# Cross attention with a mixture of experts: projection turns and VectorE's work moved between the steps, squares of the roots on GpSimd

## The reference

```python
q = layernorm(x) @ Wq.T ; k = context @ Wk.T ; v = context @ Wv.T      # (Wk and Wv interleave)
q, k = rmsnorm(q), rmsnorm(k)                                          # per head of 16
attn = softmax(einsum('bhnd,bhmd->bhnm', q, k) * 16 ** -0.5)
x = x + einsum('bhnm,bhmd->bhnd', attn, v)
x = x + moe_ffn(layernorm(x))
```

## Time and profile before

| what | value |
|---|---|
| runs of the kernel before | median 1047.12 us (1046.23 to 1047.95) |
| the profiled execution | 1044.72 us, its span 1043.0 us |
| TensorE's granted clock in it | 0.983 of full speed |
| busy over the span | PE 965.8, DVE 703.4, ACT 513.9, POOL 146.5 us |
| exponentials (L612), 128 of them | 240.5 us, mean 1879 ns |
| idle of ScalarE before them | 77.9 us, 75.1 of it ended by the scores |
| first exponential | at 41.97 us |
| MoE part | after the last unit, from about 488 us |

### The profile page before, as it was taken

The page is one execution under the profiler, slowest core; times in us unless marked ns, Lnnn a source line. Parts: engine busy times, 40 slices in busy tenths (PEclk is TensorE's granted clock), DMA queues, the critical chain, the costliest instruction groups (busy, mean ns, idle before and its releaser), DMA issues.

```text
span 1043.0 us, 17988 instructions
## 1 busy us (share of the span) xinstructions
PE 965.8 (93%) x6730; PEld 697.2 (67%) x6731; DVE 703.4 (67%) x1439; ACT 513.9 (49%) x625; POOL 146.5 (14%) x167
## 2 busy tenths in 40 slices
PE   4999999989998999976999999999999999999995
PEld 3534443345434453332998898889998998899895
DVE  6777867775687657663678675675666767757553
ACT  4577768856786568874333212422424232424211
POOL 1000000000000000001100000243233331332331
PEclk9999999999999999997899999999999999999998
DMA  9100100001000100201420118354363544553633
GB/s 336 69 1 2 41 1 1 16 6 61 1 2 21 62 1 1 102 21 41 140 83 21 41 36 270 74 180 71 62 181 71 164 83 151 131 137 69 174 61 40
DMA packets 28984, 78.93 MB, mean 76 GB/s; under 512 B 7040, under 2 KB 7040, under 8 KB 24832
## 3 DMA queue, kind: packets, MB, share of 16 engines
q1 hardware_dynamic: 18400, 52.31, 14.1%
q0 software_dynamic: 10528, 25.87, 12.7%
HBM read 57.64 MB, written 20.52 MB: 75 GB/s over the span
## 4 chain that ended last, share of the span: by engine, by line
PE 36%; DVE 8%; DMA 4%; issue 2%; ACT 1%; POOLq 0%; POOL 0%; SPq 0%; DVEq 0%; ACTq 0%
PE z_ps L1184 14%; PE u_ps L1184 10%; PE y_ps L1184 9%; DVE w_sb L1375 4%; PE xt_ps L1197 2%; DMA out<-y_sb,target 2%; DMA xg<-xn_dram,index 1%; DMA xn_dram<-dense 1%; DVE y_sb L1562 1%; DVE g_sb L1547 1%; DVE y_sb L1569 1%; DVE g_hi L1550 1%; DVE u_lo L1534 0%; PE z_ps L1178 0%; PE xt_ps L1210 0%
## 5 line engine op out<-in xcount | busy, mean ns | idle before, releaser
L612 ACT ACTIVATE probs<-scores 128x2048 f32<-128x2048 f32 x128 | 240.5, 1879 | 77.9 <-PE scores L267 75.1
L1184 PE MATMUL z_ps<-u_hi,w_sb 128*128 128x256 f32 x896 | 169.6, 287 | 6.6 <-DVE u_lo L1534 6.6
L1184 PE MATMUL u_ps<-x_hi,w_sb 128*128 128x256 f32 x896 | 167.5, 285 | 4.8 <-issue 3.0
L1313 ACT ACTIVATE u_hi<-u_ps,b_ug 128x256 fp32r<-128x256 f32 x112 | 47.1, 472 | 238.5 <-PE u_ps L1184 238.5
L1184 PEld LDWEIGHTS z_ps<-u_hi,w_sb 128*128 128x128 f32 x896 | 142.9, 193 | 8.1 <-DVE u_lo L1534 8.1
L1184 PEld LDWEIGHTS u_ps<-x_hi,w_sb 128*128 128x128 f32 x896 | 142.8, 193 | 7.6 <-issue 4.5
L1184 PE MATMUL y_ps<-w_sb,g_hi 128*128 128x512 f32 x448 | 138.7, 391 | 0.0
L283 PE MATMUL o_ps<-probs,v_sb 128*17 128x512 f32 x1024 | 137.3, 609 | 1.0 <-ACT probs L612 1.0
L1184 PE MATMUL z_ps<-u_lo,w_sb 128*128 128x256 f32 x448 | 127.4, 284 | 0.0
L1184 PE MATMUL u_ps<-x_lo,w_sb 128*128 128x256 f32 x448 | 127.4, 284 | 0.0
L267 PEld LDWEIGHTS scores<-q_st,k_hi 32*128 32x128 f32 x512 | 25.1, 183 | 124.0 <-ACT probs L612 70.5
(11 more groups left out here) (216 smaller groups left out, 1562.5 us busy)
## 6 DMA issues: line engine op xcount, KB each, us to landing
w_raw<-w_all SPq DMA_DIRECT2D x27, 1024.0 KB, 8.3
ctx_raw<-ctx_t SPq DMA_DIRECT2D x4, 1024.0 KB, 6.2
out<-x_sb SPq DMA_DIRECT2D x16, 256.0 KB
xg<-xn_dram POOLq DMA_DIRECT2D x14, 256.0 KB
x_sb<-x SPq DMA_DIRECT2D x1, 3072.0 KB, 18.7
xn_dram<-xn SPq DMA_DIRECT2D x12, 256.0 KB, 2.1
bd<-b_down SPq DMA_DIRECT2D x9, 256.0 KB
x_sb<-x SPq DMA_DIRECT2D x4, 256.0 KB, 3.5
```

The costliest lines, as they stand in the source:

```text
L612: nc.scalar.activation(probs[:, t % 2], scores[:], ACT.Exp).then_inc(p_ready, 1)
L1184: ins = nc.tensor.matmul(out_ps, stat[a], mov[b], start=(first and a + b == 0), stop=(last and a == 1), skip_group_check=True)
L1313: last = nc.scalar.activation(u_hi[:, c, :], u_ps[:, b, a, :], ACT.Identity, bias=b_ug[:, par, 0, c:c + 1])
```

## The change

TensorE: the turns of k are spread 5, 1, 4, 2 over steps 6, 7, 0, 1 and those of q 4, 5, 3 over steps 3, 4, 5. In step 6 of groups 1 to 3 of a batch with a follower the k turns stand behind `weighed`. ScalarE: `root2_q` and `root2_k` go to GpSimd as products; `square_q` goes from step 7 to 6; `norm_high` of tile 1 is gone (VectorE does `norm_both`). VectorE: `stack_q` of half 0 goes from step 3 to 4, of half 1 from step 4 to step 0 of the next unit; `newton_k` from 6 to 5; the parts of `context_split` from steps 2, 3, 4, 4 to 1, 2, 2, 3; the statistics of a coming batch from steps 0, 1, 6, 7 to 1, 2, 3, 6.

```diff
+        K_TURNS = {6: (0, 5), 7: (5, 6), 0: (6, 10), 1: (10, 12)}
+        Q_TURNS = {3: (0, 4), 4: (4, 9), 5: (9, 12)}
...
+            def root2_q(u):
+                pool.wait_ge(rq_ready, u + 1)
+                pool.wait_ge(norm_done, 2 * u if u else 1)
+                nc.gpsimd.tensor_tensor(r2[:], r0[:], r0[:], ALU.mult).then_inc(r2q_ready, 1)
+
+            def root2_k(u):
+                pool.wait_ge(rk_ready, u + 1)
+                if u:
+                    pool.wait_ge(norm_done, 2 * u + 1)
+                nc.gpsimd.tensor_tensor(r2[:], r0[:], r0[:], ALU.mult).then_inc(r2k_ready, 1)
+
             root(0, 0)
             nc.gpsimd.memset(xt2[:, 1], 0.0).then_inc(zeros_set, 1)
...
+            root2_k(0)
+            root2_q(0)
+            roots = 1
+            for u in range(UNITS):
+                b, g, more, behind = batch_of(u)
+                if u + 1 < UNITS:
+                    root2_q(u + 1)
+                if behind and g == 1:
+                    root(roots, 1)
+                    roots += 1
+                if u + 1 < UNITS:
+                    root2_k(u + 1)
...
+                if u == 0 or (g == GROUPS - 1 and b + 2 < BATCH):
+                    root(roots, 0)
+                    roots += 1
...
@@ def between(u, s): @@
+                if s in (0, 1) and u + 1 < UNITS:
+                    k_turns(u + 1, *K_TURNS[s])
...
-                elif s <= 5:
+                elif s in Q_TURNS:
                     if ahead:
-                        q_passes(u + 2, s - 3)
+                        q_turns(u + 2, *Q_TURNS[s])
...
-                    if ahead:
-                        k_chunk(u + 2, 0)
                     if behind and g == 2:
                         gates(b - 1, 0)
-                elif ahead:
-                    k_chunk(u + 2, 1)
+                    if ahead and not (more and g >= 1):
+                        k_turns(u + 2, *K_TURNS[s])
+                elif s == 7 and ahead:
+                    k_turns(u + 2, *K_TURNS[s])
                     sum_q(u + 2)
+
+            def after(u, s):
+                b, g, more, behind = batch_of(u)
+                if s == 6 and more and g >= 1:
+                    k_turns(u + 2, *K_TURNS[s])
...
@@ def before_exp(u, s): @@
                 elif s == 3:
-                    if nxt:
-                        root2_q(u + 1)
...
                 elif s == 6:
                     if more and g == 1:
                         norm_high(b + 1, 0)
-                    if nxt:
-                        root2_k(u + 1)
-                else:
-                    if more and g == 1:
-                        norm_high(b + 1, 1)
                     if u + 2 < UNITS:
                         square_q(u + 2)
...
@@ def step(u, s): @@
                 if s == 0:
-                    stat1(0)
+                    if more and g == 2:
+                        norm_both(b + 1, 2)
+                    if u:
+                        stack_q(u, 1)
                     if behind and g == 1:
                         stat(tile_of(b - 1, 2), mv2[:, 2, :])
...
                     if nxt:
                         first_root_q(u + 1)
-                elif s == 2:
                     if more and g == 2:
                         context_split(b + 1, 0)
+                    stat1(0)
+                elif s == 2:
                     if u:
                         finalize(u - 1, 1)
                     if nxt:
                         sums_k(u + 1)
+                    if more and g == 2:
+                        context_split(b + 1, 1)
+                        context_split(b + 1, 2)
...
                         newton_q(u + 1)
-                        stack_q(u + 1, 0)
                     if more and g == 2:
-                        context_split(b + 1, 1)
+                        context_split(b + 1, 3)
...
                         first_root_k(u + 1)
-                        stack_q(u + 1, 1)
+                        stack_q(u + 1, 0)
...
                     finalize(u, 0)
+                    if nxt:
+                        newton_k(u + 1)
...
                 elif s == 6:
                     if more and g == 1:
                         norm_low(b + 1, 0)
+                        norm_both(b + 1, 1)
                     if nxt:
-                        newton_k(u + 1)
                         stack_k(u + 1, 0)
...
                 else:
-                    if more and g == 1:
-                        norm_low(b + 1, 1)
...
```

More of the change, by code:

```diff
@@ L292, in three, with q_turns @@
                 return ins
-            def q_passes(u, part):
+            TURNS = [(c, a, b) for c in range(DC) for a, b in ((0, 0), (0, 1), (1, 0))]
+            def q_turns(u, first, end):
                 g = u % GROUPS
-                if part == 0:
+                if first == 0:
                     begin("b", B_AT, ("q", u), b_free)
@@ L299, in q_passes @@
                     pe.wait_ge(xt_split, (u // GROUPS + 1) * BT)
-                turns = [(c, a, b) for c in range(DC) for a, b in ((0, 0), (0, 1), (1, 0))]
-                for c, a, b in turns[4 * part:4 * part + 4]:
+                for c, a, b in TURNS[first:end]:
                     last = nc.tensor.matmul(bank_b[:], (wq_hi, wq_lo)[a][:, g, c, :], (xt_hi, xt_lo)[b][:, c, :],
@@ L304, in q_passes, with k_turns @@
                                             skip_group_check=True)
-                if part == 2:
+                if end == len(TURNS):
                     last.then_inc(b_ready, 1)
-            def k_chunk(u, c):
+            def k_turns(u, first, end):
                 g = u % GROUPS
-                if c == 0:
+                if first == 0:
                     begin("a", A_AT, ("k", u), a_free)
@@ L313, in k_chunk @@
                     pe.wait_ge(ctx_split, (u // GROUPS + 1) * MT)
-                last = three(bank_a[:], (wk_hi[:, g, c, :], wk_lo[:, g, c, :]), (ctx_hi[:, c, :], ctx_lo[:, c, :]),
-                             c == 0, c == DC - 1)
-                if c == DC - 1:
+                for c, a, b in TURNS[first:end]:
+                    last = nc.tensor.matmul(bank_a[:], (wk_hi, wk_lo)[a][:, g, c, :], (ctx_hi, ctx_lo)[b][:, c, :],
+                                            start=(c == 0 and a + b == 0), stop=(c == DC - 1 and a == 1),
+                                            skip_group_check=True)
+                if end == len(TURNS):
                     last.then_inc(a_ready, 1)
@@ L410, in between @@
                         out_transposes(u, 0)
+                        if more and g == 1:
+                            norm_transposes(b + 1, 0)
                         if more and g >= 2:
@@ L433, in _ @@
                 four_transposes(scores[:, i, :], xn[:, i, :]).then_inc(first_t, 1)
-            k_chunk(0, 2)
-            k_chunk(0, 3)
+            k_turns(0, 6, 12)
             sum_k(0)
-            for part in range(3):
-                q_passes(0, part)
+            q_turns(0, 0, 12)
             v_all(scores[:, 0, :], 0, 0).then_inc(first_v, 1)
@@ L442, in _ @@
             v_all(scores[:, 3, :], 0, 3).then_inc(first_v, 1)
-            for part in range(3):
-                q_passes(1, part)
-            k_chunk(1, 0)
-            k_chunk(1, 1)
+            q_turns(1, 0, 12)
+            k_turns(1, 0, 6)
             sum_q(1)
@@ L479, in square_q @@
                 act.wait_ge(b_ready, B_AT["q", u] + 1)
[L480 to L484 removed]
+                act.wait_ge(tr_ready, TR_AT["sum_k", max(u - 1, 0)] + 1 if u != 1 else TR_AT["sum_q", 0] + 1)
                 nc.scalar.activation(sq[:], bank_b[:], ACT.Square).then_inc(sqq_done, 1)
@@ L904, in step @@
                     if more and g == 1:
+                        norm(b + 1, 2)
+                    if behind and g == 2:
+                        norm2(b - 1, 2)
+                else:
+                    if behind and g == 2:
+                        gates_out(b - 1, 0)
+                    if u + 2 < UNITS:
+                        sums_q(u + 2)
+                    if more and g == 1:
                         norm(b + 1, 3)
+                    if nxt:
+                        stack_k(u + 1, 1)
                     if behind and g == 1:
```

68 lines of the change are left out of this document (12 added, 56 removed).

## The result

The changed kernel takes 1051.22 us (median of 19 runs, 1047.68 to 1055.33), the kernel before 1046.44 on the same chip (19 runs, 1042.2 to 1050.77): a ratio of 1.0047 [1.0033, 1.006], some 4.9 us slower. That lies inside the range, but the case held likeliest, no change, did not come about.

What follows compares the result with a forecast made beforehand. It took TensorE as near its bound on average, with loss in single steps priced by the latest of three engines. Terms 0.9 - 0.6 + 2.2 - 1.0 - 0.8 + 0.6 - 0.8 + 0 gave +0.5: median 1047.6, range 1041 to 1053.5.

Steps and rivals of the forecast that it cites:

- the case held likeliest, no change: Whole kernel: a time within 0.2% (2.1 us) of before, given chance 0.48 against faster 0.27 and slower 0.25.
- The plain units: Units 4, 8 and 12, without projection or normalisation of the next batch: 23.32 us for 23.66, together -1.0 us.
- The exchange of waits: Batch-preparing units: TensorE waits 2 to 3 us before sum_k in units 2, 6, 10; step 5's 1.80 wait goes.
- Unit 13: Unit 13: -0.34 as a plain unit, +1.0 for late sum_k and small change, together +0.6 us.
- the working's terms for the turns: Plain units: step times from respread projection turns, such as step 4 3.02 (before 2.78) and step 7 2.93 (3.40).
- Pair -0.4: Units 5 and 6, 9 and 10 alike: sum_k 2.4 us later, then -2.8 from ended waits and turns; both pairs -0.8.
- Units 1 and 2 ... +2.2: Units 1 and 2: late VectorE piece costs +2.5 us with no waits to win back; remaining steps give 0.3.
- The forecast case's own range: Whole kernel: the forecast case, chance 0.60, spans 1044 to 1051 us for unit 14, unit 0, prologue and stalls.
- the rival that GpSimd holds VectorE: Slower rival, chance 0.17: 14 products block VectorE by the shared port, up to 1.1 us each; half gives 1055 us.
- VectorE keeps up: Faster rival, chance 0.17: moved VectorE work finds gaps, 14.3 us less, 1033; half of it, in the pairs alone, 1043.
- nothing hangs on these steps: Rival, chance 0.06: moved turns and VectorE's delays are all hidden, so no change, 1047 us.
- The rule about the port: VectorE and GpSimd share a locked port; trace showed GpSimd's power at 2.98 us for 1.06, no row the reverse.

Runs made afterwards that it cites:

- e3: Kernel before with only the two squares of a unit moved from ScalarE to GpSimd as products: 1048.53 us, ratio 1.0014 to before.
- e4: Kernel before with only the changed kernel's TensorE program, the new spread of turns: 1048.08 us, ratio 1.0013 to before.
- e2: Changed kernel with two zero-weight matmuls ahead of sum_k in step 2 of units 1, 6 and 10: 1051.98 us, ratio 1.0056 to before.
- e5: Changed kernel with two zero-weight matmuls ahead of sum_k in units 1, 2, 6 and 10: 1049.02 us, ratio 1.0017 to before.
- e8: e1 with three k turns in each of steps 0 and 1 and the prologue's first two squares on ScalarE: 1042.86 us, ratio 0.995 to before.
- e11: Kernel before with only stack_q's second half moved from step 4 to step 0 of the next unit: 1064.9 us, ratio 1.0161 to before.
- e10: e9 with eight matmuls of zeros added in units 14 and 15: 1035.7 us, ratio 0.9896 to before.
- e7: Changed kernel with each GpSimd product done twice, one behind the other: 1060.99 us, ratio 1.0133 to before.
- e1: Changed kernel with stack_q's second half put back in step 4: 1043.29 us, ratio 0.9974 to before.
- e6: Changed kernel with the spread of k and q turns as before: 1052.15 us, ratio 1.005 to before.
- e9: e8 with stack_q's second half moved to step 5, ahead of finalize: 1036.9 us, ratio 0.9912 to before.

## Why the prediction was right and wrong

**Held.** The plain units, -0.99 us for -1.0. The exchange of waits: sum_k 2.24, 2.71 and 2.72 us late in units 2, 6 and 10 (2 to 3 were given) and 0.95 or 0.96 in units 5, 9 and 13 (1.0), the 1.80 and 0.82 gone. Unit 13 (+0.66 for +0.6). The product's time: 1.04 us without company (e3), 1.07 on average in after, where 1.2 was taken. In the plain units the working's terms for the turns (+0.16, +0.24, -0.23, +0.30, -0.47) add up to nothing, and step 3, by root2_q, is the whole gain; e4 (-0.03) and e3 (-0.30) bear out both. Two numbers of the working do not come out of its rows. It took 1.93 us from an exponential to the next scores where the earlier trace rows give 2.01, by which the plain unit would gain 0.26; in after it is 1.92 (162.37 to 164.29), so the working's number stood. And the prologue's lower bound is given as -0.2, while two squares of 0.62 us gone are -1.2; the sum does not use it.

**The step that failed** is the sum for the units that prepare a batch: "Pair -0.4" and "Units 1 and 2 ... +2.2". Their mechanism was right and a term was missing. The working priced every matmul behind the late sum_k at its duration before, at full clock. Behind the wait it ran at 0.51. The forecast was wrong by 6.0 - 0.5 = 5.5 us of the attention, and this is where they are:

- clock in units 1, 6 and 10: 1.54 + 1.38 + 1.28 = 4.2, by e2. Without it the pairs are 61.60 and 61.66 us in e2 against 61.83 and 61.81 before: -0.23 and -0.15, near the -0.4 forecast.
- GpSimd's hold of `wq_lo` in unit 1: 0.7. In e5, with no drop in units 1 and 2, these take 58.78 us, +3.27; less 0.7 that is +2.6, where +2.2 was forecast.
- prologue +0.4, unit 14 +0.4, units 3, 7, 11 +0.3, unit 0 +0.2: together 1.3; and what the two lines above leave over of the pairs, with unit 13, 0.8.
- unit 15, at -1.56 for 0: before had its own drop there, which after mostly lacks. Chance had a part in the total.

That 1051.2 us lies inside the range is in part luck. The forecast case's own range ended at 1051; the upper end of the whole, 1053.5, came from the rival that GpSimd holds VectorE, and that is not what made the time.

**The prologue** was priced at +0.9 and measured at +1.33. In after the first product takes 1.87 us from 25.33, beside wv_lo (2.29 us from 24.01), and newton_k's first pass waits 0.33 for it. From the start of wv_lo to that pass it is 3.23 us, before 3.01: 0.22 of the 1.33. The start of the first exponential scatters by more than the rest: with the old squares it was at 42.83, 41.10, 43.57 and 43.19 us (e8 to e11) and 41.97 (before). Nor is unit 0 alike in all: e8, e10 and e11 have no low stretch in it and take 25.7 to 25.8 us, the others 26.7 to 27.5. The two together are steadier. Unit 1 starts at 68.10 to 69.22 us in the six kernels with the old squares, at 69.71 to 70.46 in the six with one product for each, and at 71.50 in e7 with two. So the products do cost time ahead of unit 1: 0.94 us from before to after, where the forecast for prologue and unit 0 was +0.3. Which operation it passes through is open beyond the 0.22.

**The rivals.** That VectorE keeps up (1033, or 1043 in its half-way form) is false of this change. e1, the change without one move, is faster than before, but its sum_k still waits 0.78 us in unit 6, as before's does: not by that rival's mechanism, then. The forecast's argument, that the piece before sum_k has no gap, is borne out, since it was the 1.9 us of stack_q put into that piece that did not fit (e1, e11). That GpSimd holds VectorE was the right sign with a small part: 0.7 us for one product, not half of 14. In e3's order it would have been 2.2 us more in units 6 and 10. That nothing hangs on these steps is refuted by e1 and e11, 12 and 17 us of attention.

The rule about the port, of which before's trace showed one direction, is seen here in the other too: VectorE's 0.69 becomes 1.41 us and its 0.75 becomes 1.53 beside a product that began first or nearly so. The Trainium skill ("SBUF — State Buffer", Who interferes with whom) says so of VectorE operations with two SBUF inputs; the trace agrees. The Trainium skill ("GPSIMD Engine Reference", Elementwise — side-by-side cycle accounting) led to an estimate of 1.1 us for the product; 1.04 was measured.

**Left open**: when the clock drops. The same wait of 2.24 us had it behind it in e2 and not in after, 2.69 us in unit 6 of e11 and 3.00 in unit 10 of e7 did not, 1.77 in unit 1 of after did and 2.04 in unit 1 of e6 did not, and e5 and e9 have a drop without such a wait. And how much of the timed 4.9 us is the attention's: the profile gives it 6.0, and the code behind it, unchanged, scatters by 4.5.

## What to carry to other kernels

When work moves from one step to another on an engine that is late, look for the piece of work without a gap that ends in the wait, and keep out of it; the busy share of the whole unit (25.8 of 36 us) says nothing about room in it. One stack_q of 1.9 us in step 0 cost 12 us of the attention in the profiles, 7.6 us by the timed ratios. With it in step 5, a place behind what TensorE asks for next, and with the first squares and one k turn put back, the change was worth 0.9%. And a wait put on TensorE is not priced by its length alone: add what the clock may take behind it, here 1.3 to 1.5 us for a wait of 1.8 to 3.0, and some 4.8 behind one of 2.24 in unit 14; but it does not take it each time.

## What the runs showed of the hardware

- The granted clock of TensorE fell to about 0.5 at the end of single waits of 1.77 to 2.99 us or just behind them (TensorE was busy 4.15, 2.67 and 3.28 of the 6 us ahead of the three drops of after), and stayed there for 3 to 4 us, once for over 12 (e8). It stayed at 1.00 behind others of 2.24 (after), 2.69 (e11) and 3.00 us (e7), and fell once each in e5 and e9 with TensorE busy 12.00 of 12 us. It was not the same from one profile to the next for equal code (unit 6 of e9 and e10, unit 2 of after and e2). Work put into the wait kept it up in the treated places (e2).
- A GpSimd product of 128x512 from one tile, squared, takes 1.04 us, 0.4 more than ScalarE's square of 0.63. Beside VectorE each delays the other: GpSimd up to 1.87 us under a VectorE subtraction of 2048 columns, VectorE from 0.69 to 1.41 us.
